# A graph network's count matrix: plan rows of four-byte values, read into eight registers at a time

## What is computed

```python
def _L2_gnn_ref(x, edge_index, W_agg, W_root, b):
    def _sage_layer(x, src, dst, Wl, Wr, bias, n_nodes):
        msg_sum = jax.ops.segment_sum(x[src], dst, num_segments=n_nodes)
        cnt = jax.ops.segment_sum(jnp.ones((src.shape[0], 1), x.dtype), dst, num_segments=n_nodes)
        mean = msg_sum / jnp.maximum(cnt, 1.0)
        return mean @ Wl + x @ Wr + bias
    for i in range(N_LAYERS - 1):
        x = jax.nn.relu(_sage_layer(x, src, dst, W_agg[i], W_root[i], b[i], n))
    return _sage_layer(x, src, dst, W_agg[-1], W_root[-1], b[-1], n)
...
x = x + _L2_gnn_ref(h, edge_index, L2_gnn_W_agg, L2_gnn_W_root, L2_gnn_b)
```

## Time and profile before

| What | Value |
|---|---|
| median of three runs | 8583.79 us (8570.0 to 8593.24) |
| the profiled execution | 8586.09 us |
| its span in the trace | 8584.3 us |
| mean granted TensorE clock | 0.711 |
| busy in the whole span | TensorE 5052.5 us, VectorE 5173.0, GpSimd 4849.7, ScalarE 2007.6 |

### The profile page before, as it was taken

One profiled execution on the slowest core, in us unless ns is written; L12 is line 12 of the kernel. 1 busy time (PEld: TensorE's weight loads), 2 busy tenths in 40 slices (PEclk: granted clock), 3 DMA queues, 4 the chain that ended last, 5 costly groups with the idle time before them and its releaser, 6 DMA issues.

```text
span 8584.3 us, 104266 instructions
## 1 busy us (share of the span) xinstructions
PE 5052.5 (59%) x25856; PEld 3304.9 (38%) x25856; DVE 5173.0 (60%) x17135; ACT 2007.6 (23%) x3703; POOL 4849.7 (56%) x5045
## 2 busy tenths in 40 slices
PE   5655556666444544548999987353374542673532
PEld 3444433333322222224444444253342542443532
DVE  7786567777566666662000139684477862697844
ACT  6666644444234444442000000000000000100000
POOL 6777657777544444440000037777677777677774
PEclk8777767777666666678999985676555765656765
DMA  6555557777233333336878852342123321233311
GB/s 185 157 154 156 154 163 203 201 202 201 60 120 132 129 135 136 128 142 248 291 273 297 289 181 86 112 119 56 43 80 117 117 79 37 72 107 108 114 52 33
DMA packets 728922, 1217.02 MB, mean 142 GB/s; under 512 B 109340, under 2 KB 547085, under 8 KB 714832
## 3 DMA queue, kind: packets, MB, share of 16 engines
q1 hardware_dynamic: 552716, 847.76, 29.5%
q0 software_dynamic: 161120, 311.32, 14.0%
q10 hardware_dynamic: 14688, 53.48, 1.6%
HBM read 865.31 MB, written 346.85 MB: 141 GB/s over the span
## 4 chain that ended last, share of the span: by engine, by line
POOL 47%; issue 23%; PE 19%; DVE 7%; DVEq 2%; DMA 1%; ACT 1%; SPq 0%; POOLq 0%; ACTq 0%
POOL RO L997 26%; POOL RO L967 17%; PE PS L1499 12%; PE PS L1436 3%; PE PS L1456 2%; POOL nd L980 2%; POOL at_first L973 2%; DVE bn L2049 1%; DVE cut_row L2050 1%; DVE acc L1935 1%; DVE shared L2050 1%; DVEq L2045 1%; POOL acc L1014 0%; PE PS L1346 0%; DVEq L2046 0%
## 5 line engine op out<-in xcount | busy, mean ns | idle before, releaser
L997 POOL DMA_INDIRECT RO<-table,src_t x2346 | 2244.3, 957 | 1999.7 <-DMA table<-H 1251.0
L967 POOL DMA_INDIRECT RO<-table,src_t x2346 | 2262.9, 965 | 1524.5 <-issue 725.2
L1935 DVE TENSOR_TENSOR acc<-acc,PS 128x128 f32 x3910 | 1093.5, 280 | 1078.2 <-PE PS L1539 745.8
L1539 PE MATMUL PS<-RO 128*128 128x128 f32 x3060 | 686.8, 415 | 1155.6 <-DMA RO<-table,src_t 1128.5
L1539 PEld LDWEIGHTS PS<-RO 128*128 128x128 f32 x3060 | 634.1, 316 | 1201.0 <-DMA RO<-table,src_t 1175.9
L2150 DVE TENSOR_SCALAR RO<-PS,loc_t,shared 128x128 f32<-128x128 f32 x2346 | 939.8, 402 | 0.6
L1456 PE MATMUL PS<-RO 128*128 128x128 f32 x3128 | 607.6, 374 | 395.5 <-DMA RO<-table,src_t 380.8
L1456 PEld LDWEIGHTS PS<-RO 128*128 128x128 f32 x3128 | 580.4, 284 | 484.3 <-DMA RO<-table,src_t 459.3
L2049 DVE TENSOR_SCALAR bn<-work,shared 128x128 bf16<-128x128 int16 x1567 | 409.5, 261 | 489.5 <-issue 454.8
L1436 PE MATMUL PS<-shared,bn 128*128 128x392 bf16 x784 | 293.3, 459 | 687.9 <-DVE shared L2050 415.2
L1119 ACT ACTIVATE H<-PS 128x392 f32<-128x392 f32 x784 | 392.8, 501 | 893.6 <-PE PS L1436 719.9
(11 more groups left out here) (382 smaller groups left out, 8787.0 us busy)
## 6 DMA issues: line engine op xcount, KB each, us to landing
GT<-adjacency SPq DMA_DIRECT2D x126, 1792.0 KB, 7.2
adjacency<-H SPq DMA_DIRECT2D x98, 1568.0 KB
RO<-adjacency SPq DMA_DIRECT2D x42, 1792.0 KB, 7.2
RO<-table,src_t POOLq DMA_INDIRECT x4692, 3.1
staged<-RO ACTq DMA_DIRECT2D x102, 512.0 KB
H<-staged SPq DMA_DIRECT2D x102, 512.0 KB
soft_rows<-shared SPq DMA_DIRECT2D x196, 256.0 KB
H<-soft_rows SPq DMA_DIRECT2D x98, 512.0 KB, 3.9
```

The costliest lines, as they stand in the source:

```text
L967: pool.indirect_dma_start(rows[:, h * HT + j, :], None, table[k % 2], at(src_t[:, t:t + 1]))\
L997: pool.indirect_dma_start(rows[:, g % 2 * HT + j, :], None, table[k % 2], at(src_t[:, t:t + 1]))\
L1539: last = mm(PS[:, o:o + D], block[:, j * D:(j + 1) * D], onehot[:, h * HT + j, :], start=True, stop=True)
L1935: tt(at, at, window_at(k, c, j), ALU.add).then_inc(added[h], 1 if j < n - 1 else HT - n + 1)
```

## The change

The three rows of the plan become integers of four bytes. `LOAD_REGS` falls from 16 to 8, on all three engines. On ScalarE and TensorE the values loaded go through a maximum with 1 into a second set of registers, and the waits and addresses are made from those.

```diff
-LOAD_REGS = 16
+LOAD_REGS = 8
...
-        window_row, tile_row = (G[0:1, (1 + i) * (STEPS + 1):(2 + i) * (STEPS + 1)].bitcast(U16) for i in range(2))
-        done_row = G[0:1, 3 * (STEPS + 1):3 * (STEPS + 1) + WINDOWS].bitcast(U16)
+        window_row, tile_row = (G[0:1, (1 + i) * (STEPS + 1):(2 + i) * (STEPS + 1)].bitcast(I32) for i in range(2))
+        done_row = G[0:1, 3 * (STEPS + 1):3 * (STEPS + 1) + WINDOWS].bitcast(I32)
...
             done_regs = [s.alloc_register(f"done{j}") for j in range(LOAD_REGS)]
+            done_held = [s.alloc_register(f"done_held{j}") for j in range(LOAD_REGS)]
...
                         s.load(done_regs, done_row[:, w:w + LOAD_REGS])
-                        steps_done = [s.snap(r, min_val=1, max_val=STEPS) for r in done_regs]
+                        for held, r in zip(done_held, done_regs):
+                            s.reg_alu(held, r, 1, ALU.max)
+                        steps_done = [s.snap(r, min_val=1, max_val=STEPS) for r in done_held]
...
             window_regs = [pe.alloc_register(f"window{j}") for j in range(LOAD_REGS)]
+            window_held = [pe.alloc_register(f"window_held{j}") for j in range(LOAD_REGS)]
...
                     pe.load(window_regs, window_row[:, i:i + LOAD_REGS])
-                    window_of[:] = [pe.snap(r, min_val=1, max_val=WINDOWS) for r in window_regs]
+                    for held, r in zip(window_held, window_regs):
+                        pe.reg_alu(held, r, 1, ALU.max)
+                    window_of[:] = [pe.snap(r, min_val=1, max_val=WINDOWS) for r in window_held]
```

## The result

The changed kernel takes 8203.24 us (median of four runs, 8196.53 to 8204.45) where the kernel before takes 8585.96 (four runs beside it). The ratio is 0.9555, interval 0.9539 to 0.9572: 383 us less. The forecast was 8157 us, its range 8065 to 8290. The profiled execution took 8196.53 us, 389.6 less than that of before.

What follows compares the result with a forecast made beforehand. Register loads of the plan were taken to stall VectorE in the 1520 us count-matrix stage. The new stage, 981 + 30 + 60 + 20 = 1091 us, is 429 less: 8586 - 429 = 8157 us, range 8065 to 8290 (forecast's own 8090 to 8230).

Steps and rivals of the forecast that it cites:

- The 15 us put in for a lower clock: Dense layer after the stage: a lower TensorE clock taken as 0, with ±15 us put into the range.
- the slow register: Rival, plan loads: the big buffer, not the two-byte form, sets the price; 1.8 us for eight, 8353 us; 4%.
- 981 busy: VectorE in the count-matrix stage: its busy time kept as measured before, 981 us.
- 30 exposed: VectorE's plan loads: 196 x 0.15 us not covered by queued work, 30 us; bounds 0 and 159.
- 60 for TensorE: VectorE in the stage: waits for TensorE kept at 60 us; bounds 20 and 120.
- 20 of issue: VectorE in the stage: other issue, ahead of the additions, kept at 20 us.
- TensorE's own round: TensorE in the stage: busy time, loads, copies and maxima sum to 943 us, below VectorE's 1091.
- the 0.16 that I took: TensorE's eight maxima per load: 0.16 us, 31 us in all, bounds 30 to 141; hidden under VectorE's 1091 us.
- The take-over rival: Rival, stage: TensorE becomes the bound through dear maxima and a lower clock, stage 1200 us, 8266 us; 12%.
- the rival that it is kept out: Rival: VectorE's mask builds hold back GpSimd's gather descriptor work, stage at least 1154 us, 8220 us; 3%.
- A price per call: Rival, plan loads: a load costs the same whatever its count, so doubled calls make it slower, 8939 us; 3%.
- My own sign of failure: Stage, profile after: loads over 1 us, or VectorE idle behind TensorE over 120 us, would make the prediction wrong.

Runs made afterwards that it cites:

- e9: The changed kernel with the three plan rows one value, four bytes, further on; 10283.75 us, ratio 0.9894 to the kernel before.
- e8: The changed kernel with all 98 slab stores put behind the last evacuation, so none is in flight during the steps; 10629.15 us, its stage 1267 us.
- e3: The changed kernel with the maxima of TensorE and ScalarE written twice; 8205.56 us, ratio 0.955 to the kernel before.
- e4: The changed kernel with each of TensorE's plan loads written twice; 10160.71 us, ratio 0.9771 to the kernel before.
- e5: The changed kernel with each of VectorE's plan loads written twice; 10165.54 us, ratio 0.9774 to the kernel before.
- e6: The changed kernel with each slab store taking partitions 64 to 127 twice, never the plan's partition; 8296.44 us in a single run.

## Why the prediction was right, and where it was off

**The place and the sign.** The stage alone moved, by 387 us where 429 were forecast, and the dense layer's 1290 us are the same to the microsecond. The 15 us put in for a lower clock weren't needed; the granted clock of the stage rose from 0.68 to 0.74.

**The load.** Forecast 0.60 us from the neighbouring four-byte loads; the median is 0.59 to 0.60 on two engines and 0.547 on ScalarE. The reason is narrower than I gave it: four-byte loads are short only from a multiple of 16 bytes, which the step of eight values and the rows' starts happen to give. In e9 the slow register, a rival with 4%, is what happened: 1.8 us for eight. The Trainium skill's 200 ns per register (Runtime: NRT & Kernel Launch, section Instruction fetch mechanics), which made it 1.6 us by an estimate, is not the price of the aligned load here, 74 ns, and lies close to the two-byte and the shifted ones, 215 to 240 ns; no run here shows a load from HBM, of which it speaks. The prediction gave the batch of eight no worth of its own; on the second chip it costs 34 to 39 us in this form.

**The step that was mis-sized: what the loads cost VectorE.** The sum was 981 busy + 30 exposed + 60 for TensorE + 20 of issue = 1091 us. Measured by the profile's own books it is 988 + 115 + 21 = 1124, and 1133 with the 9 us between these and the stage's length (before, 4 us). The waits for TensorE are 55 above forecast, those for issue 29 below. The books mislead here as the place at 2704.22 us showed, so I trust the other count: of 141 us idle up to 93 behind VectorE's plan loads, where the forecast had 30, and 48 for all else, where it had 80. With 7 us more busy and 4 at the stage's ends that is +63 - 32 + 7 + 4 = 42 us, the stage's 1133 against 1091. The exposed loads were taken up to three times too small, still inside the bounds of 0 to 159. Behind loads of up to 0.7 us stand 25 us, near the 30 of the forecast; the other 68 stand behind longer ones. The reason is the load's spread: the mean on VectorE is 1.07 us, not 0.60, since every load that meets a store takes up to three times as long. The row was there to see: the four-byte load of this very stage stands in the earlier trace rows as 594/606/1987, and I took the median and didn't ask what its maximum was. The plan loads of before had the same spread, 3.8 us at the least and 6.7 at the median: a load came every sixteen steps and a store every eight windows, some sixteen steps too, so nearly all of TensorE's met one (94 of 98, counted; the four others took 3.78 to 3.98 us). By e8 a load without a store stays below 0.8 us. So the change took from the loads both their own time, by the form, and much of the time that they spent under a store: over their shortest time TensorE's loads stood 264 us before (634 - 98 x 3.78) and 52 after (167 - 196 x 0.587).

**TensorE's own round.** Forecast 943 us. It is 796 busy + 167 of loads + 51 of maxima + 196 x 0.038 = 1021, still below 1133. The maxima are two fused operations per load and not one, 0.26 us against the 0.16 that I took, 51 us against 31, within the bounds of 30 to 141. The waits view has its matmuls wait 227 us for VectorE's masks (L2056), but 146 of these overlap TensorE's own loads, so they don't prove slack either. That the maxima cost the kernel nothing is argued from the sum of 1021 us; no run shows it, since e3's second set did not run. Nor does a run show that VectorE and not TensorE is the bound, since the second loads of e4 and e5 did not run. The take-over rival (8266 us) didn't come.

**GpSimd.** The median gather is 944 ns as before, with VectorE 87% busy, and GpSimd still waits 207 us for TensorE; the rival that it is kept out didn't come. The Trainium skill's lock (SBUF — State Buffer, section SBUF: two separate sides) doesn't show in the median. The gathers' busy time did rise from 665.28 to 700.45 us for the same 697, by some longer ones (the maximum from 1.73 to 2.23 us); whether VectorE, the stores or TensorE's faster pace does that was not tried, and nothing waits for it.

**A price per call.** Excluded: eight values cost 0.59 us and sixteen 1.10.

**My own sign of failure.** I wrote that loads over 1 us, or more than 120 us behind TensorE, would make the prediction wrong. The first came, on two fifths of VectorE's loads, and the second nearly, 115 us. Both are signs of the one mis-sized term; the price was 42 us, which the bounds of that term had covered.

## What to carry to other kernels

Look for register loads before any engine's busy time when a stage is filled by nobody: in the profile they stand as issue, as a wait for an engine that was done, or as TENSOR_LOAD on a sequencer. Keep rows that are loaded to registers as four-byte values, begin every load at a multiple of 16 bytes, and keep the loads away from large stores. Try the length of a load again once its form has changed: halving it gained 149 us with two-byte values and lost 34 to 39 with four-byte ones. When an experiment repeats an instruction, count it in the trace before you read the time: in e3, e4 and e5 the repeated one was not there. When a duration is taken over from a neighbouring row, take its mean or ask what its maximum is, not its median alone.

## What the hardware did that I had not expected

- A load of eight four-byte values from the big buffer takes 0.59 us from a multiple of 16 bytes and 1.76 to 1.94 us from four bytes beyond it; 17 or 18 values took 1.36 us at the least from such a multiple and 4.03 at the least from elsewhere. Two-byte values cost the same as the unaligned ones: 1.72 to 1.92 us for eight.
- A slab store in flight makes such a load up to three times as long on VectorE and TensorE (0.60 to 1.8 us within the store; 2.1 at most), also when the store reads partitions 64 to 127 alone (e6); the gathers in flight alone don't (0.773 us at most, e8), and a transfer into the buffer at 395 GB/s doesn't slow ScalarE's load of four registers (0.284 and 0.311 us), where one out of it at 393 GB/s does (0.905 and 0.909). None of ScalarE's plan loads in the changed kernel was slow (0.555 us at most), and none ended less than 8.2 us after a store was issued, so none met one; in the kernel before 48 of its 49 did, and took 4.90 to 6.61 us where the other took 3.41.
- Eight register maxima take 0.26 us on TensorE's sequencer, as two fused operations of 85 and 175 ns.
- The same kernel (before) took 8594 us on one chip and 10392 and 10400 on two others, and the changed kernel 8203 against 10148 and 10161 to 10166, with the same median register loads.
